# Rotary attention: the output halves go through ScalarE and GpSimd instead of VectorE, and GpSimd's passes change their order

## The reference

```python
qkv = xn @ w_qkv                                   # xn: normed twice, gamma and beta
q, k, v = heads of 64
q, k = rope(q), rope(k)                            # t * cos + rot(t) * sin; row 0 as it is
attn = softmax(q @ k.T * 64 ** -0.5)
x = x + (attn @ v, heads side by side) @ w_out
```

## Time and profile of before

| | us |
|---|---|
| median of 3 runs (lowest, highest) | 1382.55 (1376.21, 1385.33) |
| the profiled execution, its own time | 1383.71 |
| its span, first to last instruction | 1382.0 |
| granted TensorE clock over the span | 0.898 |
| VectorE's adds L593, in all | 240 in the loop at 339 ns |

### The profile page before, as it was taken

One profiled execution on the slowest core, in us unless ns is written; L12 is line 12 of the kernel. 1 busy time (PEld: TensorE's weight loads), 2 busy tenths in 40 slices (PEclk: granted clock), 3 DMA queues, 4 the chain that ended last, 5 costly groups with the idle time before them and its releaser, 6 DMA issues. The chain is left out here.

```text
span 1382.0 us, 33990 instructions
## 1 busy us (share of the span) xinstructions
PE 1134.8 (82%) x13103; PEld 745.8 (54%) x13104; DVE 995.5 (72%) x1625; ACT 698.8 (51%) x1102; POOL 396.4 (29%) x215
## 2 busy tenths in 40 slices
PE   2898989889898989899898942793589999999885
PEld 1565666666566656666565632462465445554443
DVE  6888898888888888988888842353575667666517
ACT  3565556656555665656565413231315556455543
POOL 0563456355435635553562003003000000000000
PEclk8899999999999999999999985797757989899997
DMA  5855454545545554555555306111154111110001
GB/s 155 213 129 134 117 139 108 142 118 128 141 121 124 125 136 114 133 129 129 125 130 136 79 21 221 40 47 44 58 171 154 48 47 48 47 37 13 17 2 36
DMA packets 66147, 140.19 MB, mean 101 GB/s; under 512 B 13233, under 2 KB 36146, under 8 KB 61874
## 3 DMA queue, kind: packets, MB, share of 16 engines
q1 hardware_dynamic: 64674, 135.86, 38.5%
q0 software_dynamic: 1424, 3.67, 0.9%
HBM read 64.71 MB, written 22.61 MB: 63 GB/s over the span
## 5 line engine op out<-in xcount | busy, mean ns | idle before, releaser
L501 ACT ACTIVATE a_probs<-a_score,a_negmax 128x1024 f32<-128x1024 f32 x256 | 285.6, 1115 | 317.2 <-DVE a_negmax L579 316.8
L579 DVE TENSOR_REDUCE a_negmax<-a_score 128x1 f32<-128x1024 f32 x256 | 309.4, 1209 | 102.0 <-PE a_score L395 102.0
L1486 DVE TENSOR_REDUCE a_lowest<-a_score 128x1 f32<-128x512 f32 (+3 forms) x320 | 181.7, 629 | 85.3 <-PE a_score L1374 44.6
L1456 ACT ACTIVATE a_probs_T<-a_score_T 128x1024 f32<-128x1024 f32 (+1 forms) x192 | 146.5, 810 | 137.7 <-PE a_score_T L1350 98.9
L407 PE MATMUL a_acc<-a_probs_Ta,a_v_repa 32*64 32x256 f32 x4096 | 152.5, 440 | 29.7 <-DVE residual L593 29.7
L585 DVE STREAM_TRANSPOSE a_probs_Tb<-a_probs 128x1024 f32<-128x1024 f32 x128 | 157.0, 1226 | 0.1
L585 DVE STREAM_TRANSPOSE a_probs_Ta<-a_probs 128x1024 f32<-128x1024 f32 x128 | 156.9, 1225 | 0.0
L407 PE MATMUL a_acc<-a_probs_Tb,a_v_repb 32*64 32x256 f32 x4096 | 127.9, 384 | 31.6 <-ACT a_k_raw L494 28.1
L395 PE MATMUL a_score<-a_k_stackah,a_q_stacka 128*128 128x512 f32 x256 | 132.8, 519 | 16.9 <-DMA a_q_stacka<-a_q_lo 14.3
L407 PEld LDWEIGHTS a_acc<-a_probs_Ta,a_v_repa 32*64 32x64 f32 x4096 | 98.0, 152 | 75.5 <-issue 55.2
L395 PE MATMUL a_score<-a_k_stackbh,a_q_stackb 128*128 128x512 f32 x256 | 114.3, 446 | 13.6 <-ACT a_probs L501 13.6
(11 more groups left out here) (236 smaller groups left out, 1906.2 us busy)
## 6 DMA issues: line engine op xcount, KB each, us to landing
a_v_repa<-rows_v SPq DMA_DIRECT2D x64, 256.0 KB, 4.3
a_v_repb<-rows_v SPq DMA_DIRECT2D x64, 256.0 KB, 4.7
a_xn_cur<-normed_T SPq DMA_DIRECT2D x17, 512.0 KB, 3.4
a_q_rot<-a_q_raw SPq DMA_DIRECT2D x68, 128.0 KB, 2.3
a_k_rot<-a_k_raw SPq DMA_DIRECT2D x68, 128.0 KB, 2.3
rows_v<-a_v_stage SPq DMA_DIRECT2D x68, 128.0 KB, 2.4
a_k_stackah<-a_k_stackah SPq DMA_DIRECT2D x16, 256.0 KB, 2.8
a_k_stackal<-a_k_stackal SPq DMA_DIRECT2D x16, 256.0 KB, 2.9
```

The source lines that it names most:

```text
L501: nc.scalar.activation(probs[s % 2][:], score_ps[s % 2][:], ACT.Exp, bias=negmax[:, s:s + 1], accum_out=den[:, s:s + 1]).then_inc(probs_re ...
L579: nc.vector.tensor_reduce(negmax[:, s:s + 1], score_ps[s % 2][:], axis=AX.X, op=ALU.max, negate=True)\
L1456: nc.scalar.activation(probs_T[k % 4][:, 2 * hp:2 * hp + 2, 0:hi - lo], score_T_ps[n % 2][:, :, 0:hi - lo], ACT.Exp).then_inc(pair_free, 1)
L1486: nc.vector.tensor_reduce(to, src, axis=AX.X, op=ALU.max, negate=True).then_inc(bank_free, 1)
```

## The change

- VectorE's `add_projected` is gone. ScalarE gets `keep_projected`: four ACTIVATE Copy of 128x128 for each half, out of PSUM into a new SBUF buffer `scaled` (two of them), scaled by the same reciprocal, a [128, 1] operand. GpSimd adds a half to the residual with one TENSOR_TENSOR of 128x512, two for each head.
- The projection and its evacuation stand at r = 6 (half 0) and r = 7 (half 1), behind the slot's item. TensorE's values wait for `out_kept` instead of `added`; ScalarE waits for `added` before it writes `scaled` again.
- Items 2 and 3 both stand in slot 0; slot 1 has none (in the loop; before the loop the slots are as they were).
- High parts of head b move from slots 15 and 0 to slots 1 and 2.
- GpSimd begins with the rotation of the second pair, and then in each iteration: `rest` of head a; the two adds of head a; cos and sin passes of q for the pair after next; `rest` of head b; the sum of q; cos, sin and sum of k; the two adds of head b. It runs as two hardware loops, one a batch.
- SP reloads `wo` of head a ahead of swapping q, and stacks b behind swapping k.

The diff, cut to its core:

```diff
+        scaled = [sb(f"scaled{i}", [P, 4, D]) for i in range(2)]
-        ITEM_SLOTS = {14: (2, 0), 15: (2, 1), 0: (1, 2), 1: (1, 3), 6: (1, 4), 7: (1, 5)}
+        ITEM_SLOTS = {14: (2, (0,)), 15: (2, (1,)), 0: (1, (2, 3)), 6: (1, (4,)), 7: (1, (5,))}
+        OUT_SLOTS = (6, 7)
...
 @block.sync
                     load_v(0, bass.ds(next_rows, 32))
+                    sp.wait_ge(projected, a_projected)
+                    load_wo(0, bass.ds(wo_row[0], DH0))
                     sp.wait_ge(item_kept, q_kept)
                     sp.wait_ge(summed[0], pairs)
                     swap_halves(0)
-                    stack(1, pairs)
-                    sp.wait_ge(projected, a_projected)
-                    load_wo(0, bass.ds(wo_row[0], DH0))
                     sp.wait_ge(item_kept, k_kept)
                     sp.wait_ge(summed[1], pairs)
                     swap_halves(1)
+                    stack(1, pairs)
...
 @block.gpsimd
+                def add_group(h, p, batch):
+                    for j in range(2):
+                        pool.wait_ge(out_kept, count(p, 4, 2 * h + 3 + j))
+                        rows = core.x[:, batch * TB + 4 * j:batch * TB + 4 * j + 4, :]
+                        nc.gpsimd.tensor_tensor(rows, rows, scaled[j][:], ALU.add).then_inc(added, 1)
+                for i in range(2):
+                    scale(i, (None, 1))
+                    total(i, (None, 1))
+                for batch in range(B):
+                    with pool.Fori(batch * HP, min(batch * HP + HP, PAIRS - 1)) as it:
+                        now, p, later = (it, 0), (it, 1), (it, 2)
+                        pool.wait_ge(summed[1], count(p, 1, 1))
+                        pool.wait_ge(added, count(now, 4, 2))
+                        for i in (1, 0):
+                            rest(0, i, p)
+                        pool.wait_ge(lo_ready[0][0], count(p, 1, 1))
+                        add_group(0, now, batch)
+                        scale(0, later)
+                        pool.wait_ge(rotated[0], count(later, 2, 2))
+                        for i in (1, 0):
+                            rest(1, i, p)
+                        pool.wait_ge(lo_ready[1][0], count(p, 1, 1))
+                        total(0, later)
+                        scale(1, later)
+                        total(1, later)
+                        add_group(1, now, batch)
+                for h in range(2):
+                    add_group(h, (None, PAIRS - 1), B - 1)
...
 @block.tensor
                         if r == PV_SLOTS[0]:
-                            pe.wait_ge(added, count(p, 4, 2 * h))
+                            pe.wait_ge(out_kept, count(p, 4, 2 * h))
-                    if r == 7 and not (first and h == 0) and not (tail and h == 1):
-                        project_out(1 - h, 0)
-                    if r == 0 and not first:
-                        project_out(h, 1)
...
+                    if r in OUT_SLOTS and group_before(s, first, tail):
+                        pe.wait_ge(attn_kept, count(p, 4, 2 * h))
+                        pe.wait_ge(wo_loaded[1 - h], count(p, 32, 32 * h))
+                        project_out(1 - h, OUT_SLOTS.index(r))
...
 @block.scalar
+                def keep_projected(h, j):
+                    for t in range(4):
+                        ins = nc.scalar.activation(scaled[j][:, t, :], acc_ps[:, j, t * P:t * P + P], ACT.Copy, scale=rden[h][:, 4 * j + t:4 * j + t + 1])
+                    ins.then_inc(out_kept, 1)
...
+                    if r in OUT_SLOTS and group_before(s, first, tail):
+                        j = OUT_SLOTS.index(r)
+                        act.wait_ge(rden_ready, count(p, 2, h))
+                        act.wait_ge(added, count(p, 4, 2 * h - 1 + j))
+                        act.wait_ge(projected, count(p, 4, 2 * h + 1 + j))
+                        keep_projected(1 - h, j)
...
-                    if s == 15 and not (tail or last):
-                        high_part(1, 1)
-                    if s == 0 and not (first or tail):
-                        high_part(1, 0)
+                    if s in (1, 2) and not (first or tail):
+                        act.wait_ge(scores_ready, count(p, SLOTS, 0))
+                        high_part(1, 2 - s)
...
 @block.vector
-                def add_projected(h, j, batch):
...
-                    if r == 0 and not first:
-                        dve.wait_ge(rden_ready, count(p, 2, h - 1))
-                        dve.wait_ge(projected, count(p, 4, 2 * h - 1))
-                        add_projected(h, 0, batch)
-                    if r == 1 and not first:
-                        dve.wait_ge(projected, count(p, 4, 2 * h))
-                        add_projected(h, 1, batch)
```

More of the change, by code:

```diff
@@ L217, in first_bank, with items_at, group_before @@
             return score_ps[k // 2][:, k % 2 * 512:k % 2 * 512 + 512] if k < 4 else acc_ps[:, k - 2, :]
[L219 to L224, removed]
+        def items_at(s, first, last, tail):
+            return (0, ()) if tail or last else (FIRST_ITEM_SLOTS if first else ITEM_SLOTS).get(s, (0, ()))
+        def group_before(s, first, tail):
+            return not (first and s < TB) and not (tail and s >= TB)
         with nc.Block() as block:
@@ L348, in _, with scale @@
                     .then_inc(slots_cleared, 16)
-                def rotate(i, p):
-                    pool.wait_ge(lo_ready[1][0], count(p, 1, 0))
+                def scale(i, p):
                     pool.wait_ge(swapped[i], count(p, 64, 64))
@@ L428, in slot @@
                         scores((s + 1) % SLOTS)
-                    if r in PV_SLOTS and not (first and h == 0) and not (tail and h == 1):
+                    if r in PV_SLOTS and group_before(s, first, tail):
                         if r == PV_SLOTS[0]:
@@ L437, in slot @@
                         values(1 - h, range(k * chunk, k * chunk + chunk), r == PV_SLOTS[-1])
-                    if r == 7 and not (first and h == 0) and not (tail and h == 1):
-                        pe.wait_ge(attn_kept, count(p, 4, 2 * h))
-                        pe.wait_ge(wo_loaded[1 - h], count(p, 32, 32 * h))
-                        project_out(1 - h, 0)
-                    if r == 0 and not first:
-                        project_out(h, 1)
-                    item = item_at(p, s, first, last, tail)
-                    if item is not None:
-                        j, n = item
-                        if first and j < 4:
-                            pe.wait_ge(item_kept, ITEMS + max(j - 2, 0) + (1 if j >= 2 else 0))
-                        elif first:
-                            pe.wait_ge(item_kept, ITEMS + j - 1)
+                    ahead, items = items_at(s, first, last, tail)
+                    for j in items:
+                        if first:
+                            pe.wait_ge(item_kept, ITEMS + max(j - 1, 0))
                         elif j in (2, 3):
@@ L457, in slot @@
                         if j == 0:
-                            ahead = 1 if first else 2
                             pe.wait_ge(w_loaded, count(p, 16, 16 * ahead + 16))
@@ L520, in slot @@
                         exponentials((s + 1) % SLOTS)
-                    if r == PV_SLOTS[-1] and not (first and h == 0) and not (tail and h == 1):
+                    if r == PV_SLOTS[-1] and group_before(s, first, tail):
                         act.wait_ge(pv_done, count(p, 2, h))
@@ L524, in slot @@
                         keep_attention()
-                    item = item_at(p, s, first, last, tail)
-                    if item is not None:
-                        j, n = item
-                        act.wait_ge(item_ready, count(p, ITEMS, ITEMS * ((FIRST_ITEM_SLOTS if first else ITEM_SLOTS)[s][0]) + j + 1))
+                    ahead, items = items_at(s, first, last, tail)
+                    for j in items:
+                        act.wait_ge(item_ready, count(p, ITEMS, ITEMS * ahead + j + 1))
                         if j in (0, 2):
-                            ahead = (FIRST_ITEM_SLOTS if first else ITEM_SLOTS)[s][0]
                             act.wait_ge(summed[j // 2], count(p, 1, ahead))
@@ L603, in slot @@
                         row_max((s + 1) % SLOTS)
[L604 to L611 removed]
+                    if r == 1 and group_before(s, first, tail):
                         dve.wait_ge(probs_ready, count(p, SLOTS, TB * h))
+                        if not first:
+                            dve.wait_ge(out_kept, count(p, 4, 2 * h - 2))
                         nc.vector.reciprocal(rden[1 - h][:], den[:, TB * (1 - h):TB * (1 - h) + TB]).then_inc(rden_ready, 1)
```

25 lines of the change are left out of this document (4 added, 21 removed).

## The result

| | before | after |
|---|---|---|
| median (lowest, highest), us | 1383.94 (1376.21, 1388.68), 4 runs | 1312.67 (1310.70, 1315.37), 4 runs |
| after / before | | 0.949 (0.944 to 0.954) |
| profiled execution: own time, span | 1383.71, 1382.0 | 1312.95, 1309.9 |

The forecast was 1314 in 1302 to 1342. In the rows of after L521 is the exponentials, L607 the maxima, L421 the scores, L433 the values, L441 the output projection, L537 the new copies on ScalarE, L377 the new adds on GpSimd.

The account below looks back on a forecast made before the run. No engine is full, so the order bounds the kernel. Per pair -4.8 + 0.3 = -4.5 us, 15 times -67.5, tail -1: from 1383.7 to 1315.2, less 1.2 for the median, 1314 us; range 1302 to 1342.

Parts of the forecast that it names:

- Slots 14 to 6: From the maximum opening slot 14 to the one opening slot 6: 21.35 us instead of 23.46, gain 2.1.
- the item ahead of a projection half: On TensorE in slots 14 and 15: an item costs 0.46 us before the next start.
- The wait of the values at slot 2: TensorE's wait of 1.9 us a pair for ScalarE's copy of item 3 goes.
- Slots 6 to 14: From the maximum opening slot 6 to the one opening slot 14: 21.74 us instead of 24.42, gain 2.7.
- ScalarE's copies: Four scaled copies of a projection half take 1.05 us of ScalarE, with ends of 0.67 and 1.48.
- GpSimd and SP: Queue chain to the copy of b's low part: issued about 20.0 us after slot 14 opens, landing at 22.9.
- I charge 0.3 us: Charge per pair for the b stack landing between 0.5 us early and 0.5 late for slot 8's scores.
- Clock: TensorE keeps 2.4 GHz, as its idle time ahead of slot 11's scores, some 1.6 us, is less than before.
- Rival 1: TensorE's clock still falls at slot 10: 1.6 us a pair, 24 in all, 1338 us; chance 0.15.
- The range: Forecast's own: copies at 0.67 us and no lateness give -5.1 a pair, 1305; copies at 1.48 us give 1322.
- Tail: Values of the last head wait 3.53 us for VectorE's eight adds; net 1 us gained.
- Rival 2: The b stack is 1 to 2 us late, slot 7 waits once a pair: 15 to 30 us, 1330 to 1345; chance 0.14.

Follow-up runs that it names:

- plain_copy: The changed kernel with each half copied by one unscaled 128x512 ACTIVATE instead of four scaled 128x128, the softmax division left out: 1311.0 us, ratio 0.948.
- rest_b_first: The changed kernel with GpSimd's two low-part passes of head b moved ahead of q's cos and sin passes: 1314.8 us, ratio 0.951.

## Why the prediction was right

The period was forecast at 43.4 us and is 43.31; the sum was right in size and, for the most part, in its terms. That it is right to 0.1 us is in part luck: without GpSimd the forecast had 43.09, to which 0.36 us came in slots 14 to 6, from which 0.15 went in slots 6 to 14, and to which the forecast had added 0.3 for a lateness that is not there.

- *Slots 14 to 6.* Forecast 21.35, measured 21.71. The scores of slot 1 start 4.57 us after the slot opens (381.65), not 4.08. The mis-sized term is the item ahead of a projection half: half 0 starts 0.96 us behind the start of item 0 and not 0.55, half 1 0.85 us behind item 1 and not 0.46. The forecast's 0.46 was the distance from an item to scores; those scores then took 1.32 us to the next start and not 1.13, and part of the item lay there. The end of the `attn_T` copies (377.47) can explain at most the 0.1 us by which the first distance exceeds the second. A half and scores behind it were each 0.1 us cheaper than forecast. The wait of the values at slot 2 is gone as said; with item 3 put back it returned with 1.55 us.
- *Slots 6 to 14.* Forecast 21.74, measured 21.59. The scores of slot 11 were to start 8.35 us in and start at 8.20.
- *ScalarE's copies.* One takes 0.381 us and four take 1.10 us of the engine (383.02 to 384.12), between my 1.05 and the 1.17 that I had estimated from the Trainium skill (ScalarE: Activation LUTs, section What ACT_TABLE_LOAD costs). The exponentials behind the copies of slot 15 start at 384.12, with their maximum ready at 382.86 + 1.23 = 384.09: the copies end just when they are needed. Cheaper ones gain nothing, as plain_copy shows; at 1.17 us they would have been late by up to 0.07, an estimate of 1 us for the whole loop.
- *GpSimd and SP.* The copy was to be issued 20.0 us after slot 14 opens and is issued at 20.34; the cos pass starts at 10.79 and not 10.0, and the passes up to the copy then take 9.5 us and not 10. The adds take 1.28 us each and are hidden. The passes kept their 2.38 us. The term that fails is "I charge 0.3 us": rest_b_first gives nothing for a stack 3 us sooner. The scores of slot 8 that it was measured against start at 23.49 and not 23.05, late mainly by the item term, and so the copy, at 23.3 by its median, lands ahead of them.
- *Clock.* Kept at its upper level through the loop, as assumed. Rival 1 did not come, with 1.5 us of idle time at slot 9.
- *The range.* With copies at 0.67 us the forecast's own chain saves 0.15 us a pair, as the maximum of slot 1 is ready at 6.54; without lateness that is -4.94 and 1307, where it says -5.1 and 1305. Nothing hung on it.
- *Tail.* 1 us forecast, 1.25 measured. The values of the last head start after 2.28 us of idle time instead of 3.53; 1.1 us at the first pair and 2.0 us in untouched stages were in no term.
- *Rival 2* had its mechanism right and its price too low beyond 2 us: it counted the wait and not the clock behind it. With 1 to 2 us of lateness I gave 15 to 30 us; measured are 19 us for 1.2 and 58 us for 2.3. A stack just one GpSimd pass later would have put the time at 1371, outside the range. Between the forecast and that stood a slack of about 0.1 us; the forecast had said "no slack", and that the b stack fell on the good side of it was luck.

The wait for the clock in the old kernel was priced rightly at 1.6 us, but taking it away by filling gave only 11 of 24 us, since another wait took over its role in 8 of 15 pairs. In the change the whole 1.6 us came through (slots 10 and 11, 6.78 to 5.20 us). Whether it needed both waits to go is not shown: with item 3's wait back at 1.55 us the clock stayed up.

## What to carry to other kernels

When an operation sits between a maximum and its exponentials, or holds PSUM banks that the next group needs, count it by the waits that it causes and not by its busy time: here the same adds cost ScalarE and GpSimd 65 and 81 us of work, where VectorE had 65, and the kernel still gains 71. Before moving a pass in a queue, write down the slack of what leaves it: a transfer with 10 us of slack became one with 0.1, and from there on a single further pass of 2.4 us costs 58 us. Waits that stand behind one another must be removed together; remove the first alone and the second shows.

## What was not expected of the hardware

- The clock answers to more than the longest wait. In the kernel before, a wait of 1.9 us at slot 2 never brought it down, while 2.0 us at slot 10 always did, with 0.7 us of idle time shortly ahead of it; once slot 10 was filled, the same wait at slot 2 did so in 8 of 15 pairs. With item 3 moved in that kernel, the wait of 1.97 us at slot 10 did so in 12 of 15. A wait of 1.2 us in slot 7 never did; of the 15 waits of 2.2 to 2.7 us there 12 did, and the longest, 2.69, did not. Each fall cost 1.5 to 1.7 us.
- With the adds back on VectorE the lower level lasts 6.8 us in every second pair instead of 3.4. The runs do not show why.
